# The experts' down product with the gated product as weights, on one Trainium2 core

## Chip, cores and metric

The kernel runs on one core of a Trainium2 chip. The metric is the device time of one execution in microseconds; lower is better. Names of engines: TensorE (PE in the rows; PEld is its weight load), VectorE (DVE), ScalarE (ACT), GpSimd (POOL), SyncE (SP, which starts transfers).

## What is computed

Four layers follow one another on x of 4 x 1024 tokens with 128 features. Each adds its result to x: banded attention, feed-forward, attention with a softmax over the heads, and the same feed-forward again. The change lies in the feed-forward, cut here to what matters:

```python
# x: 4096 tokens x 128, normalised; 32 experts with 64 inner features, 8 are chosen per token
g = einsum('th,eih->eti', x, expert_gate)
u = einsum('th,eih->eti', x, expert_up)
outs = einsum('eti,ehi->eth', silu(g) * u, expert_down)
final = sum over the 8 chosen experts of topk_w * outs
shared = (silu(x @ shared_gate.T) * (x @ shared_up.T)) @ shared_down.T
x = x + final + shared
```

## The kernel before

`feed_forward` runs twice, as ffn1 and ffn2, each time over 8 blocks of 512 tokens. All 32 experts are computed for all tokens, two at a time (a pair fills the 128 rows), with the share of experts that were not chosen set to zero. With the shared expert that makes 17 units in a block (`NU`), unit 0 of a block being the shared one, and 136 units in a stage. What follows calls the units of a block g = 0 to 16.

Float32 values are kept as two float16 parts, high and low, and each product is three matmuls: high by high, high by low, low by high. `product` (lines 112 to 116) does so with the expert's weights loaded into the array and 512 tokens streamed. For each unit:

- TensorE makes `gate` and `up` (three matmuls each, 128x512, features on the partitions).
- ScalarE makes `sg` = silu(gate) (L1443). GpSimd multiplies it by the tokens' shares of that expert into `sw` (L1332). VectorE multiplies `sw` by `up` into `hidden` (L1583, for the shared expert L1586).
- ScalarE copies `hidden` to its high part (L1448), VectorE subtracts to the low part (L1591), both into `h_parts`, which has three buffers.
- TensorE makes `down` from `h_parts` three units later (`LAG` = 3), and adds up all 17 units of a block in one PSUM bank, `down`.

After a block `down` holds the features on the partitions, and x has the tokens there. So ScalarE copies `down` to `dT` (`take_down`, L1453), TensorE turns it with four float32 transposes into a second bank, `back` (`turn_back`, L1389), and VectorE adds `back` to x (`add_back`, L1596).

The order is written out by hand, engine by engine, and engines wait for one another at counting semaphores. TensorE's loop does for each unit: gate, up, then down of the unit three before. So the last down of a block (g = 16) falls into g = 2 of the next block, behind up; after it stand the four transposes of the next block's shares (`turn_weights`, L1362). In g = 3 come gate, up and the first down of the new block, which in the kernel before waits for `dT_ready` (ScalarE has emptied the bank), and then `turn_back`. VectorE adds in its iteration g = 4. Its other work, the choice of experts for coming blocks (`route`), lies in g = 5 to 15, and in block 0 at double rate.

Of the kernel before, what the change touches and what calls it, by code (L numbers as in the profile page):

```python
# [16 lines left out]
ALU = mybir.AluOpType  # L17
ACT = mybir.ActivationFunctionType
AX = mybir.AxisListType

P = 128
B, S, E = 4, 1024, 128
# [5 lines left out]
BLK = 512  # L28
NBLK = T // BLK
TB = BLK // P  # L30
# [21 lines left out]
NPAIR = NEXP // 2  # L52
# [4 lines left out]
WSCALE = 16.0  # L57
ASCALE = 4.0
NU = NPAIR + 1
ONE = 1  # L60
# [51 lines left out]
def product(pe, out, w, i, hi, lo, start=True, stop=True):  # L112

    pe.matmul(out, w[:, i, 0, :], hi, start=start, stop=False)  # L114
    pe.matmul(out, w[:, i, 0, :], lo, start=False, stop=False)  # L115
    return pe.matmul(out, w[:, i, 1, :], hi, start=False, stop=stop)  # L116
# [1094 lines left out]
def feed_forward(nc, stage, c, x, mv, w_dram, stats_next, out=None):  # L1211
# [10 lines left out]
    LAG = 3  # L1222
    STATS = {NU - 1: range(2), 0: range(2, TB)}
    with Mem(nc, stage) as m:
# [10 lines left out]
        wide = m.sb("wide", [P, 2, NPAIR, BLK])  # L1235
        sg, sw = m.sb("sg", [P, 2, BLK]), m.sb("sw", [P, 2, BLK])
        h_parts = m.sb("h_parts", [P, LAG, 2, BLK], F16)
        dT = m.sb("dT", [P, BLK])
        stats = m.sb("stats", [P, TB, 6])
        gate, up, hidden = m.ps("gate", [P, 2, BLK]), m.ps("up", [P, 2, BLK]), m.ps("hidden", [P, 2, BLK])  # L1240
        down, back = m.ps("down", [P, BLK]), m.ps("back", [P, BLK])
# [6 lines left out]
        weights_ready, pt_ready, wT_ready = m.sem("weights_ready", "dve"), m.sem("pt_ready", "pe"), m.sem("wT_ready", "act")  # L1248
# [2 lines left out]
        gate_ready, up_ready, sg_ready = m.sem("gate_ready", "pe"), m.sem("up_ready", "pe"), m.sem("sg_ready", "act", 1)  # L1251
        sw_ready, h_ready = m.sem("sw_ready", "pool"), m.sem("h_ready", "dve", 1)
        high_ready, low_ready, down_done = m.sem("high_ready", "act"), m.sem("low_ready", "dve", 1), m.sem("down_done", "pe", LAG - 1)
        dT_ready, back_ready, added = m.sem("dT_ready", "act"), m.sem("back_ready", "pe"), m.sem("added", "dve")
        out_stored = m.sem("out_stored", "sp")
        block = m.ctx.enter_context(nc.Block())

# [8 lines left out]
        def part_of(unit):  # L1266

            return NPAIR if unit % NU == 0 else unit % NU - 1
# [65 lines left out]
        @block.tensor  # L1334
        def _(pe):
            m.start(pe, "pe")

            def turn(k):
                pe.wait_ge(xn_ready, ONE + k + 1)
                if k > 3:  # L1340
                    pe.wait_ge(xlow_ready, ONE + k - 3)
                    pe.wait_ge(xs_ready, ONE + k - 3)
                for j in range(TB):
                    last = pe.transpose(turned(k)[:, j * P:(j + 1) * P], xn[:, k % 2, j, :], c["ident"][:, :])  # L1344
                last.then_inc(turned_ready, 1)

            def logits_of(k):
                pe.wait_ge(xs_ready, ONE + k + 1)
                pe.wait_ge(logits_read, ONE + k)
                for j in range(TB):  # L1350
                    last = pe.matmul(logits[:, k % 2, j * NEXP:(j + 1) * NEXP], xs[:, k % 2, j * P:(j + 1) * P],  # L1351
                                     c["gate_w"][:, :], start=(j == 0), stop=True, skip_group_check=True)
                last.then_inc(logits_ready, 1)

            def turn_weights(k):
                pe.wait_ge(weights_ready, ONE + k + 1)
                if k > 0:
                    pe.wait_ge(wT_ready, ONE + k)
                if k > 2:
                    pe.wait_ge(added, ONE + k - 2)  # L1360
                for j in range(TB):
                    last = pe.transpose(back[0:NEXP, j * P:(j + 1) * P], weights[:, j, :], c["ident"][:, :])  # L1362
                last.then_inc(pt_ready, 1)

            def gate_of(unit):
                k, i = unit // NU, part_of(unit)
                xh, xl = xnT[:, 0, k * BLK:(k + 1) * BLK], xnT[:, 1, k * BLK:(k + 1) * BLK]
                pe.wait_ge(sg_ready, ONE + unit)
                product(pe, gate[:, unit % 2, :], c["gate_parts"], i, xh, xl).then_inc(gate_ready, 1)

            def up_of(unit):
                k, i = unit // NU, part_of(unit)
                xh, xl = xnT[:, 0, k * BLK:(k + 1) * BLK], xnT[:, 1, k * BLK:(k + 1) * BLK]
                pe.wait_ge(h_ready, ONE + unit)
                product(pe, up[:, unit % 2, :], c["up_parts"], i, xh, xl).then_inc(up_ready, 1)

            def down_of(unit):
                pe.wait_ge(low_ready, ONE + unit + 2)
                if unit % NU == 0:
                    pe.wait_ge(dT_ready, ONE + unit // NU)  # L1380
                product(pe, down[:, :], c["down_parts"], part_of(unit), h_parts[:, unit % LAG, 0, :], h_parts[:, unit % LAG, 1, :],
                        start=(unit % NU == 0), stop=(unit % NU == NPAIR)).then_inc(down_done, 1)

            def turn_back(k):
                pe.wait_ge(dT_ready, ONE + k + 1)
                pe.wait_ge(added, ONE + k)
                pe.wait_ge(wT_ready, ONE + min(k + 3, NBLK))
                for j in range(TB):
                    last = pe.transpose(back[:, j * P:(j + 1) * P], dT[:, j * P:(j + 1) * P], c["ident"][:, :])  # L1389
                last.then_inc(back_ready, 1)  # L1390

            for k in range(NBLK):
                turn(k)
                if k > 0:
                    logits_of(k - 1)
                if k == 3:
                    turn_weights(0)
            logits_of(NBLK - 1)
            pe.wait_ge(xlow_ready, ONE + NBLK)
            pe.wait_ge(xs_ready, ONE + NBLK)  # L1400
            for unit in range(UNITS + LAG):
                if unit < UNITS:
                    gate_of(unit)
                    if unit == 0:
                        pe.wait_ge(logits_read, ONE + NBLK + 1)
                    up_of(unit)
                if unit >= LAG:
                    down_of(unit - LAG)
                if turned_at(unit) is not None:
                    turn_weights(turned_at(unit))  # L1410
                if unit % NU == LAG and unit > NU:
                    turn_back(unit // NU - 1)
            turn_back(NBLK - 1)

        @block.scalar
        def _(act):
# [30 lines left out]
                act.wait_ge(down_done, ONE + unit)  # L1447
                act.activation(h_parts[:, unit % LAG, 0, :], hidden[:, unit % 2, :], ACT.Copy).then_inc(high_ready, 1)  # L1448

            def take_down(k):  # L1450
                act.wait_ge(down_done, ONE + (k + 1) * NU + LAG - 1)
                act.wait_ge(back_ready, ONE + k)
                act.activation(dT[:, :], down[:, :], ACT.Copy, scale=1 / WSCALE).then_inc(dT_ready, 1)  # L1453

            for k in range(NBLK):
                split_turned(k)
                if k > 0:
# [5 lines left out]
            for unit in range(UNITS):  # L1463
                gate_of(unit)
                if unit > 0:
                    high_part(unit - 1)
                if unit % NU == LAG - 1 and unit > NU:
                    take_down(unit // NU - 1)
                if turned_at(unit) is not None:
                    take_weights(turned_at(unit))  # L1470
            high_part(UNITS - 1)
            take_down(NBLK - 1)

        @block.vector
        def _(dve):
# [100 lines left out]
            def hidden_of(unit):  # L1576

                dve.wait_ge(up_ready, ONE + unit + 1)
                dve.wait_ge(low_ready, ONE + unit)
                h, upu = hidden[:, unit % 2, :], up[:, unit % 2, :]  # L1580
                if part_of(unit) < NPAIR:
                    dve.wait_ge(sw_ready, ONE + weighed_before(unit) + 1)
                    dve.tensor_tensor(h, sw[:, unit % 2, :], upu, ALU.mult).then_inc(h_ready, 1)  # L1583
                else:
                    dve.wait_ge(sg_ready, ONE + unit + 2)
                    dve.scalar_tensor_tensor(h, sg[:, unit % 2, :], 1 / WSCALE, upu, ALU.mult, ALU.mult).then_inc(h_ready, 1)  # L1586
# [4 lines left out]
                dve.tensor_tensor(h_parts[:, unit % LAG, 1, :], hidden[:, unit % 2, :], h_parts[:, unit % LAG, 0, :], ALU.subtract).then_inc(low_ready, 1)  # L1591

            def add_back(k):
                dve.wait_ge(back_ready, ONE + k + 1)
                xt = x[:, k * TB:(k + 1) * TB, :]
                dve.tensor_tensor(xt, xt, back[:, :].rearrange("p (t e) -> p t e", t=TB), ALU.add).then_inc(added, 1)  # L1596

            def stats_of(k, tiles):
                dve.wait_ge(added, ONE + k + 1)
# [22 lines left out]
            for unit in range(UNITS + 1):  # L1622
                if unit < UNITS:
                    hidden_of(unit)
                if unit > 0:
                    low_part(unit - 1)
                if unit % NU == LAG + 1 and unit > NU:
                    add_back(unit // NU - 1)
                k, pieces = pieces_at(unit)
                for piece in pieces:  # L1630
                    route(k, piece)
                if stats_next and unit > NU and unit % NU in STATS:
                    k = (unit + 1) // NU - 2
                    if k >= 0:
                        stats_of(k, STATS[unit % NU])
# [118 lines left out]
```

## Time and profile before

| | us |
|---|---|
| median of 3 runs (2033.71 to 2040.03) | 2039.27 |
| profiled execution, its time | 2041.47 |
| profiled execution, its span from first to last instruction | 2039.7 |
| TensorE busy | 1922.7 (94%) |
| VectorE busy | 1726.2 (85%) |
| GpSimd busy | 1512.7 (74%) |
| ScalarE busy | 1242.0 (61%) |

The two feed-forward stages lie at about 246 to 548 us and 1735 to 2040 us of the span. The mean granted clock of TensorE is 0.966 of full speed, and 1.00 inside the steady part of both. In the rows below a matmul's time runs from its start to its modelled end, so that the rows of a stream overlap; the pace is the distance between two starts.

### The profile page before, as it was taken

To read this page: it belongs to the slowest core of one execution; us is meant where nothing else is said; L and a number is where in the kernel's file an instruction comes from. 1 tells how busy PE (TensorE), PEld (TensorE's weight loads), DVE (VectorE), ACT (ScalarE), POOL (GpSimd) and SP (SyncE) were. 2 spreads that over 40 slices of the span, in tenths; PEclk is the share of its full clock that TensorE was granted. 3 is DMA by queue.
4 is the path that set the end of the run, shared out by engine and by line. 5 is a ranking of instruction groups with operands and counts; after the bars stand their busy time and mean duration, and the time that the engine had idled before them with its cause. 6 is when DMAs were issued, how large, how long until landed. Compare 5 with 4: busy or idle time off the path is not lost. (4 is left out here: it accounts for less than half of the span.)

```text
span 2039.7 us, 54384 instructions
## 1 busy us (share of the span) xinstructions
PE 1922.7 (94%) x21688; PEld 1277.0 (63%) x21688; DVE 1726.2 (85%) x2642; ACT 1242.0 (61%) x2225; POOL 1512.7 (74%) x1104
## 2 busy tenths in 40 slices
PE   5888799999889999999999999999999998899998
PEld 3566554444357777777777777777777776544443
DVE  6656688887689999999999999999999997788876
ACT  4446456666546666666666666666666665566665
POOL 5126035555359999999999999999999997256565
PEclk8989889999879999999999999999999999799999
DMA  7755167857120000000000000000000000578763
GB/s 194 205 126 128 31 125 132 157 126 134 68 79 13 14 9 18 9 14 14 13 15 9 17 10 14 13 11 16 6 10 6 9 6 2 87 157 152 131 130 60
DMA packets 119885, 125.83 MB, mean 62 GB/s; under 512 B 32208, under 2 KB 82272, under 8 KB 118896
## 3 DMA queue, kind: packets, MB, share of 16 engines
q1 hardware_dynamic: 114112, 117.65, 27.5%
q10 hardware_dynamic: 5520, 4.70, 0.8%
q8 instruction: 172, 2.82, 0.6%
q14 instruction: 81, 0.66, 0.1%
HBM read 101.71 MB, written 20.69 MB: 60 GB/s over the span
## 5 line engine op out<-in xcount | busy, mean ns | idle before, releaser
L1098 DVE TENSOR_REDUCE head_shift<-head_score 128x64 bf16<-128x1024 f32 x512 | 624.4, 1220 | 80.7 <-PE head_score L882 68.6
L1055 ACT ACTIVATE head_ex<-head_score 128x1024 f32<-128x1024 f32 x512 | 524.7, 1025 | 185.4 <-PE head_score L904 183.7
L839 POOL TENSOR_TENSOR head_half<-head_ex 128x1024 f32<-128x1024 f32 x256 | 604.1, 2360 | 40.7 <-ACT head_ex L1055 40.7
L1332 POOL TENSOR_TENSOR ffn_sw<-ffn_sg,ffn_wide 128x512 f32<-128x512 f32 x256 | 324.6, 1268 | 300.2 <-ACT ffn_sg L1443 283.0
L1105 DVE TENSOR_TENSOR head_ex<-head_ex,head_recp 128x1536 f32<-128x1536 f32 x256 | 446.7, 1745 | 4.2 <-ACT head_recp L1027 4.2
L914 PE MATMUL head_den<-head_half,c_ident 128*128 128x128 f32 x3072 | 385.4, 275 | 2.4 <-POOL head_half L840 2.4
L914 PEld LDWEIGHTS head_den<-head_half,c_ident 128*128 128x128 f32 x3072 | 363.4, 192 | 6.0 <-POOL head_half L840 2.6
L846 POOL TENSOR_TENSOR head_ex<-head_ex,head_recip 128x512 f32<-128x512 f32 x256 | 328.6, 1284 | 21.3 <-ACT head_recip L1029 12.9
L904 PE MATMUL head_score<-head_shift,c_identb 128*128 128x512 bf16 x1024 | 309.9, 384 | 17.9 <-DVE head_shift L1098 11.7
L882 PE MATMUL head_score<-att_b_HB,att_b_GR 96*128 96x256 f16 x2048 | 310.9, 274 | 1.1 <-issue 0.6
L897 PE MATMUL head_outp<-head_ex,att_b_vs 128*32 128x128 f32 x8192 | 276.5, 276 | 0.6 <-DVE head_ex L1105 0.6
L897 PEld LDWEIGHTS head_outp<-head_ex,att_b_vs 128*32 128x32 f32 x8192 | 208.1, 109 | 108.4 <-issue 107.4
L1583 DVE TENSOR_TENSOR ffn_hidden<-ffn_sw,ffn_up 128x512 f32<-128x512 f32 x256 | 178.1, 696 | 94.4 <-POOL ffn_sw L1332 85.5
L882 PEld LDWEIGHTS head_score<-att_b_HB,att_b_GR 96*128 96x128 f16 x2048 | 200.1, 98 | 81.5 <-ACT head_ex L1055 2.9
L1443 ACT ACTIVATE ffn_sg<-ffn_gate 128x512 f32<-128x512 f32 x272 | 162.1, 596 | 116.9 <-PE ffn_gate L116 115.7
L1448 ACT ACTIVATE ffn_h_parts<-ffn_hidden 128x512 f16<-128x512 f32 x272 | 162.2, 596 | 97.4 <-DVE ffn_hidden L1583 90.9
L840 POOL TENSOR_TENSOR head_half<-head_half 128x256 f32<-128x256 f32 x256 | 185.5, 725 | 20.1
L1024 ACT ACTIVATE head_lnd<-head_den 128x128 f32<-128x128 f32 x256 | 71.1, 278 | 206.8 <-PE head_den L914 206.8
L1591 DVE TENSOR_TENSOR ffn_h_parts<-ffn_hidden,ffn_h_parts 128x512 f16<-128x512 f32 x272 | 186.0, 684 | 0.1
L904 PEld LDWEIGHTS head_score<-head_shift,c_identb 128*128 128x128 bf16 x1024 | 72.2, 98 | 88.7 <-DVE head_shift L1098 79.6
L114 PE MATMUL ffn_down<-ffn_h_parts,c_down_parts 128*128 128x512 f16 x272 | 103.2, 379 | 3.3 <-DVE ffn_h_parts L1591 3.3
L114 PE MATMUL ffn_up<-ffn_xnT,c_up_parts 128*128 128x512 f16 x272 | 104.2, 383 | 0.4 <-DVE ffn_hidden L1583 0.2
(264 smaller groups left out, 2466.3 us busy)
## 6 DMA issues: line engine op xcount, KB each, us to landing
ffn_wide<-pair_weights SPq DMA_DIRECT2D x256, 256.0 KB, 9.7
band_v_windows<-a_values SPq DMA_DIRECT2D x24, 384.0 KB, 6.5
att_b_vs<-in_zero_f SPq DMA_DIRECT2D x2, 2176.0 KB, 9.0
a_values<-band_v_rows ACTq DMA_DIRECT2D x8, 512.0 KB, 5.7
a_keys<-band_parts_k SPq DMA_DIRECT2D x12, 295.5 KB, 2.8
att_a_HB<-a_keys SPq DMA_DIRECT2D x48, 73.9 KB
a_queries<-band_parts_q SPq DMA_DIRECT2D x12, 271.5 KB, 3.1
att_a_GR<-a_queries SPq DMA_DIRECT2D x12, 271.5 KB
```

Source lines behind the costliest of these rows:

```text
L114: pe.matmul(out, w[:, i, 0, :], hi, start=start, stop=False)
L839: ch.link(pool.tensor_tensor(hf, e[:, 0:8, :], e[:, 8:16, :], ALU.add))
L846: pool.tensor_tensor(e, e, recip[:, kt % 2, :][:, None, :].broadcast_to([P, NG, P]), ALU.mult).then_inc(rest_ready, 1)
L882: last = pe.matmul(score[:, h, g // 2, (g % 2) * GH * QS:(g % 2 + 1) * GH * QS].rearrange("p (a w) -> p a w", a=GH), GR[:, buf, g, kt * P: ...
L897: last = pe.matmul(outp[g * 32:(g + 1) * 32, 0:P], vs[:, buf * BT + kt, at:at + 32], ex[:, kt % RING, n, :], start=(kt == 0 and n4 == 0), ...
L904: last = pe.matmul(score[:, h, k, :].rearrange("p (a w) -> p a w", a=NH // 2), c["identb"][:, :], shift[:, h, :][:, None, :].broadcast_to( ...
L914: last = pe.matmul(den[:, 0:P], c["ident"][:, :], half[:, kt % 2, k, :], start=(i == 0), stop=(i == len(SLABS) - 1))
L1055: act.activation(ex[:, kt % RING, :, h * QS:(h + 1) * QS], score[:, h, :, :].rearrange("p k (a w) -> p (k a) w", a=NH // 2), ACT.Exp, scal ...
L1098: dve.tensor_reduce(shift[:, h, :], score[:, h, :, :].rearrange("p k (a w) -> p w k a", a=NH // 2), AX.XY, ALU.max, negate=True).then_inc( ...
L1105: dve.tensor_tensor(e, e, recp[:, 0:P][:, None, None, :].broadcast_to([P, NG, ON_DVE, P]), ALU.mult).then_inc(prob_ready, 1)
L1332: pool.tensor_tensor(sw[:, unit % 2, :], sg[:, unit % 2, :], wide[:, k % 2, i, :], ALU.mult).then_inc(sw_ready, 1)
L1591: dve.tensor_tensor(h_parts[:, unit % LAG, 1, :], hidden[:, unit % 2, :], h_parts[:, unit % LAG, 0, :], ALU.subtract).then_inc(low_ready, 1)
```

## The change

The down product changes its two operands. A piece of 128 tokens of `h_parts` is now loaded as weights, and the expert's down weights (128 columns) are streamed. The result has the tokens on the partitions and the features in the columns. A unit takes four pieces by three matmuls of 128 columns in place of three matmuls of 512. `take_down` and `turn_back` are gone, and with them `dT`, `dT_ready` and `back_ready`. VectorE adds `down` to x itself, with the scale in the same instruction. It does so in its iteration g = 2, between `hidden` of that unit and the low part of the unit before. The first down of a block waits for `added` instead of `dT_ready`.

```diff
             def down_of(unit):
+                w, i, parts = c["down_parts"], part_of(unit), h_parts[:, unit % LAG, :, :]
+                first, final = unit % NU == 0, unit % NU == NPAIR
                 pe.wait_ge(low_ready, ONE + unit + 2)
-                if unit % NU == 0:
-                    pe.wait_ge(dT_ready, ONE + unit // NU)
-                product(pe, down[:, :], c["down_parts"], part_of(unit), h_parts[:, unit % LAG, 0, :], h_parts[:, unit % LAG, 1, :],
-                        start=(unit % NU == 0), stop=(unit % NU == NPAIR)).then_inc(down_done, 1)
-
-            def turn_back(k):
-                pe.wait_ge(dT_ready, ONE + k + 1)
-                pe.wait_ge(added, ONE + k)
-                pe.wait_ge(wT_ready, ONE + min(k + 3, NBLK))
+                if first:
+                    pe.wait_ge(added, ONE + unit // NU)
                 for j in range(TB):
-                    last = pe.transpose(back[:, j * P:(j + 1) * P], dT[:, j * P:(j + 1) * P], c["ident"][:, :])
-                last.then_inc(back_ready, 1)
+                    high, low, out = parts[:, 0, j * P:(j + 1) * P], parts[:, 1, j * P:(j + 1) * P], down[:, j * E:(j + 1) * E]
+                    pe.matmul(out, high, w[:, i, 0, :], start=(first and j == 0), stop=False, skip_group_check=True)
+                    pe.matmul(out, high, w[:, i, 1, :], start=False, stop=False, skip_group_check=True)
+                    last = pe.matmul(out, low, w[:, i, 0, :], start=False, stop=final, skip_group_check=True)
+                last.then_inc(down_done, 1)
...
-                if unit % NU == LAG and unit > NU:
-                    turn_back(unit // NU - 1)
-            turn_back(NBLK - 1)
...
-            def take_down(k):
-                act.wait_ge(down_done, ONE + (k + 1) * NU + LAG - 1)
-                act.wait_ge(back_ready, ONE + k)
-                act.activation(dT[:, :], down[:, :], ACT.Copy, scale=1 / WSCALE).then_inc(dT_ready, 1)
...
             def add_back(k):
-                dve.wait_ge(back_ready, ONE + k + 1)
+                dve.wait_ge(down_done, ONE + (k + 1) * NU + LAG - 1)
                 xt = x[:, k * TB:(k + 1) * TB, :]
-                dve.tensor_tensor(xt, xt, back[:, :].rearrange("p (t e) -> p t e", t=TB), ALU.add).then_inc(added, 1)
+                dve.scalar_tensor_tensor(xt, down[:, :].rearrange("p (t e) -> p t e", t=TB), 1 / WSCALE, xt, ALU.mult, ALU.add).then_inc(added, 1)
...
                     hidden_of(unit)
+                if unit % NU == LAG - 1 and unit > NU:
+                    add_back(unit // NU - 1)
                 if unit > 0:
                     low_part(unit - 1)
-                if unit % NU == LAG + 1 and unit > NU:
-                    add_back(unit // NU - 1)
```

What stands on VectorE around the border of two blocks, from `hidden` of g = 1 on (`ffn_sw` by `ffn_up` is `hidden`, `ffn_h_parts` the low part, `x_tokens` is x). Before:

```order
L1583 TENSOR_TENSOR ffn_hidden<-ffn_sw,ffn_up 128x512
L1591 TENSOR_TENSOR ffn_h_parts<-ffn_hidden,ffn_h_parts 128x512
L1583 TENSOR_TENSOR ffn_hidden<-ffn_sw,ffn_up 128x512
L1591 TENSOR_TENSOR ffn_h_parts<-ffn_hidden,ffn_h_parts 128x512
L1583 TENSOR_TENSOR ffn_hidden<-ffn_sw,ffn_up 128x512
L1591 TENSOR_TENSOR ffn_h_parts<-ffn_hidden,ffn_h_parts 128x512
L1583 TENSOR_TENSOR ffn_hidden<-ffn_sw,ffn_up 128x512
L1591 TENSOR_TENSOR ffn_h_parts<-ffn_hidden,ffn_h_parts 128x512
L1596 TENSOR_TENSOR x_tokens<-x_tokens,ffn_back 128x512
```

And in the change (L1569 is `hidden`, L1577 the low part, L1582 the addition):

```order
L1569 TENSOR_TENSOR ffn_hidden<-ffn_sw,ffn_up 128x512
L1577 TENSOR_TENSOR ffn_h_parts<-ffn_hidden,ffn_h_parts 128x512
L1569 TENSOR_TENSOR ffn_hidden<-ffn_sw,ffn_up 128x512
L1582 SCALAR_TENSOR_TENSOR x_tokens<-ffn_down,x_tokens 128x512
L1577 TENSOR_TENSOR ffn_h_parts<-ffn_hidden,ffn_h_parts 128x512
```

The addition has moved up by two iterations and stands directly behind `hidden` of g = 2.

TensorE at the same border, from the last matmul of up in g = 3 to the gate of g = 4. Before:

```order
L116 MATMUL ffn_up<-ffn_xnT,c_up_parts 128x512
L114 MATMUL ffn_down<-ffn_h_parts,c_down_parts 128x512
L115 MATMUL ffn_down<-ffn_h_parts,c_down_parts 128x512
L116 MATMUL ffn_down<-ffn_h_parts,c_down_parts 128x512
L1389 MATMUL ffn_back<-c_ident,ffn_dT 128x128 x4
L114 MATMUL ffn_gate<-ffn_xnT,c_gate_parts 128x512
```

In the change:

```order
L116 MATMUL ffn_up<-ffn_xnT,c_up_parts 128x512
L1384 MATMUL ffn_down<-c_down_parts,ffn_h_parts 128x128
L1385 MATMUL ffn_down<-c_down_parts,ffn_h_parts 128x128
L1386 MATMUL ffn_down<-c_down_parts,ffn_h_parts 128x128
```

These three stand four times, twelve matmuls in a unit, and behind them comes the gate of g = 4 at once: the four transposes of L1389 are gone.

## Rows read from the trace of the kernel before

**Rows 1.** The page's first line: the span.

```profile
span 2039.7 us, 54384 instructions
```

**Rows 2.** Busy time by stretch: PE, PEld, DVE, ACT, POOL, clock, DMA share, GB/s.

```profile
1850.00:1950.00 100.00, 100.00 (x477) 46.70 (x475) 82.44 (x204) 61.53 (x107) 59.82 (x48) 1.00 0.78 141
```

**Rows 3.** Timeline of PE from block 3's first down: start, duration, instruction.

```profile
378.81 0.38 PE L114 MATMUL ffn_down<-ffn_h_parts,c_down_parts 128*128 128x512 f16 x1
...
379.45 0.60 PE L1389 MATMUL ffn_back<-c_ident,ffn_dT 128*128 128x128 f32 x4
379.89 0.38 PE L114 MATMUL ffn_gate<-ffn_xnT,c_gate_parts 128*128 128x512 f16 x1
...
383.77 0.38 PE L114 MATMUL ffn_gate<-ffn_xnT,c_gate_parts 128*128 128x512 f16 x1
```

**Rows 4.** Timeline of PE, first and last of 24 matmuls in the attention's start.

```profile
20.55 0.22 PE L361 MATMUL band_score<-c_a_parts,att_a_xnT 128*128 128x128 f16 x1
...
21.83 0.22 PE L363 MATMUL band_score<-c_a_parts,att_a_xnT 128*128 128x128 f16 x1
```

**Rows 5.** Instructions on the bank `down`: count, ns min/median/max, first and last start.

```profile
L114 PEld LDWEIGHTS ffn_down<-ffn_h_parts,c_down_parts x272: 95/98/98, 275.8 to 2034.1; 128*128 128x128 f16 x136
```

**Rows 6.** The same columns, for two lines of VectorE.

```profile
L1586 DVE SCALAR_TENSOR_TENSOR ffn_hidden<-ffn_sg,ffn_up x16: 685/695/697, 271.1 to 1999.9; 128x512 f32<-128x512 f32 x16
L1596 DVE TENSOR_TENSOR x_tokens<-x_tokens,ffn_back x16: 676/679/689, 316.2 to 2036.3; 128x512 f32<-128x512 f32 x16
```

**Rows 7.** Timeline of DVE at the start of block 3.

```profile
378.06 0.70 DVE L1583 TENSOR_TENSOR ffn_hidden<-ffn_sw,ffn_up 128x512 f32<-128x512 f32 x1 [0.55 <-POOL ffn_sw L1332]
378.66 0.68 DVE L1591 TENSOR_TENSOR ffn_h_parts<-ffn_hidden,ffn_h_parts 128x512 f16<-128x512 f32 x1
...
384.02 0.68 DVE L1596 TENSOR_TENSOR x_tokens<-x_tokens,ffn_back 128x512 f32<-128x512 f32 x1
```

**Rows 8.** Timelines of ACT and POOL at the start of block 3.

```profile
375.98 0.60 ACT L1443 ACTIVATE ffn_sg<-ffn_gate 128x512 f32<-128x512 f32 x1 [0.43 <-PE ffn_gate L116]
...
377.44 0.59 ACT L1453 ACTIVATE ffn_dT<-ffn_down 128x512 f32<-128x512 f32 x1
...
376.65 1.27 POOL L1332 TENSOR_TENSOR ffn_sw<-ffn_sg,ffn_wide 128x512 f32<-128x512 f32 x1 [0.62 <-ACT ffn_sg L1443]
```

**Rows 9.** Timelines of PE and DVE at the starts of blocks 1 and 7.

```profile
311.01 0.38 PE L114 MATMUL ffn_down<-ffn_h_parts,c_down_parts 128*128 128x512 f16 x1
...
311.12 0.68 DVE L1591 TENSOR_TENSOR ffn_h_parts<-ffn_hidden,ffn_h_parts 128x512 f16<-128x512 f32 x1
...
513.95 0.38 PE L114 MATMUL ffn_down<-ffn_h_parts,c_down_parts 128*128 128x512 f16 x1
...
514.25 0.68 DVE L1591 TENSOR_TENSOR ffn_h_parts<-ffn_hidden,ffn_h_parts 128x512 f16<-128x512 f32 x1
```

**Rows 10.** Timelines at the ends of ffn1 and ffn2.

```profile
544.45 0.38 PE L116 MATMUL ffn_down<-ffn_h_parts,c_down_parts 128*128 128x512 f16 x1
...
546.28 0.69 DVE L1596 TENSOR_TENSOR x_tokens<-x_tokens,ffn_back 128x512 f32<-128x512 f32 x1 [1.65 <-PE ffn_back L1389]
...
2034.51 0.38 PE L116 MATMUL ffn_down<-ffn_h_parts,c_down_parts 128*128 128x512 f16 x1
2034.93 0.60 ACT L1453 ACTIVATE ffn_dT<-ffn_down 128x512 f32<-128x512 f32 x1 [1.64 <-PE ffn_down L116]
...
2036.27 0.69 DVE L1596 TENSOR_TENSOR x_tokens<-x_tokens,ffn_back 128x512 f32<-128x512 f32 x1 [2.26 <-PE ffn_back L1389]
```

**Rows 11.** Timelines of PE and DVE in and just behind block 0 of ffn1.

```profile
289.11 0.61 PE L1362 MATMUL ffn_back<-c_ident,ffn_weights 128*32 128x128 f32 x4 [0.40 <-DVE ffn_weights L1564]
...
307.24 0.69 DVE L1586 SCALAR_TENSOR_TENSOR ffn_hidden<-ffn_sg,ffn_up 128x512 f32<-128x512 f32 x1
...
307.48 0.38 PE L116 MATMUL ffn_gate<-ffn_xnT,c_gate_parts 128*128 128x512 f16 x1
307.98 0.39 PE L114 MATMUL ffn_up<-ffn_xnT,c_up_parts 128*128 128x512 f16 x1
```

More of the change, by code:

```diff
@@ L1237, in feed_forward @@
         h_parts = m.sb("h_parts", [P, LAG, 2, BLK], F16)
-        dT = m.sb("dT", [P, BLK])
         stats = m.sb("stats", [P, TB, 6])
@@ L1253, in feed_forward @@
         high_ready, low_ready, down_done = m.sem("high_ready", "act"), m.sem("low_ready", "dve", 1), m.sem("down_done", "pe", LAG - 1)
-        dT_ready, back_ready, added = m.sem("dT_ready", "act"), m.sem("back_ready", "pe"), m.sem("added", "dve")
+        added = m.sem("added", "dve")
         out_stored = m.sem("out_stored", "sp")
@@ L1466, in _ @@
                     high_part(unit - 1)
-                if unit % NU == LAG - 1 and unit > NU:
-                    take_down(unit // NU - 1)
                 if turned_at(unit) is not None:
@@ L1471, in _ @@
             high_part(UNITS - 1)
-            take_down(NBLK - 1)
         @block.vector
```

## The prediction

> **What bounds the kernel now.** I read the page first, then the busy time by stretch, then the timelines of the four engines around one border between blocks. The span is 2039.7 us [rows 1]. In the middle of ffn2 TensorE is busy for all of a 100 us stretch, at a granted clock of 1.00, its full level of 2.4 GHz, while VectorE has 82 us of work and GpSimd 60 [rows 2]. So in both feed-forward stages TensorE's own stream is the bound, and every us of work or waiting that is put into that stream counts in full. The pace of the stream: from the gate at 379.89 to the gate at 383.77 lie 18 matmuls of 512 columns, 3.88 us or 0.2156 us each [rows 3]. A unit of nine is 1.94 us. Outside these stages nothing changes.
>
> **The down product.** Three matmuls of 512 columns take 3 x 0.2156 = 0.647 us. The new form, twelve matmuls of 128 columns with twelve weight loads, stands in the trace already: the values of the first attention are made with the same three-matmul pattern, and 24 of them start from 20.55 to 21.83, 1.28 us over 23 distances or 0.0557 us each [rows 4]. Twelve take 0.668 us. The columns are the same in number (1536), and each instruction adds a little over 2 ns, nine more of them per unit: +0.021 us. The weight load's own duration of 98 ns [rows 5] does not show in that pace. This counts in 232 of the 272 units. In block 0 of each stage VectorE sets the pace at several places: TensorE waits there for the shares at 289.11 (0.40 us idle) and for `hidden` before the up at 307.98, half a us behind the gate at 307.48 where 0.216 would do [rows 11]. A slower down uses up these waits, so I leave its 17 units out, and the last three of a stage, which wait for VectorE anyway. 232 x 0.021 = +4.9 us. Bounds: 0.019 per unit if the pace is 0.0555, which gives +4.3, and all of block 0 counted too, +5.6.
>
> **The transposes.** `turn_back` goes from TensorE's stream. It starts at 379.45 and the next gate at 379.89 [rows 3]: 0.44 us, seven times in each stage, 14 x 0.44 = -6.2 us. Its wait for `dT` cost nothing there, since it starts 0.64 us behind the first down as three matmuls ask. ScalarE's copy (0.59 us, [rows 8]) had cover, and is worth nothing inside the stage.
>
> **The wait that takes their place.** Before, ScalarE emptied the bank at 377.44 to 378.03 [rows 8], and the first down of the new block at 378.81 found it free [rows 3]. Now it waits until VectorE has added, and VectorE stands in `hidden` of g = 2 first. That one comes late: it needs `sg` (375.98), then `sw` on GpSimd (376.65, 1.27 us), and starts at 378.06 [rows 7, 8]. These are one chain from the gate, which the change leaves as it is. The instruction behind it starts at 378.66 [rows 7]. In the change this is the addition. No row has it in its new form; the nearest ones are the same operation on 128x512 with one PSUM operand, 0.695 us, and the present addition, 0.679 [rows 6]. I take 0.69, and 0.05 to reach TensorE, which is what it took from the end of L1586 at 307.93 to the up at 307.98 [rows 11]. So the down can start at 378.66 + 0.74 = 379.40. TensorE gets there at 378.81 + 0.02 (a longer down before it) = 378.83, and stands 0.57 us. Nothing can overtake: gate of g = 4 is queued behind it. That is the price for blocks 2 to 6, which look alike in both stages: 10 x 0.57 = 5.7 us. At block 1 it is 311.12 + 0.74 - 311.03 = 0.83, at block 7, where no `turn_weights` gives time, 514.25 + 0.74 - 513.97 = 1.02 [rows 9]; both stages, 2 x (0.83 + 1.02) = 3.7. Together +9.4 us. Bounds: 9.0 with 0.02 less per wait, 10.8 if the first weight load behind each wait, no longer hidden, adds its 98 ns [rows 5].
>
> The low part of g = 1 slides back by 0.6 us, to end at about 379.95. Its down is due at 379.40 + 0.668 + 1.29 = 381.36, so it has 1.4 us of cover. The addition at 384.02 [rows 7] leaves VectorE's iteration g = 4, where it held up nobody.
>
> **The ends.** Behind the last down of a stage the chain was ScalarE, TensorE, VectorE: from 2034.93 to the addition at 2036.27, 1.34 us [rows 10]. In ffn1 the last down ends at 544.83, and a hand-over of 0.04 as in ffn2 puts the start at 544.87; the addition came at 546.28, so 1.41. The addition now starts at once. The last down is 0.02 longer, twice. -2.7 us, bounds -2.5 and -2.8.
>
> **The sum.** +4.9 - 6.2 + 9.4 - 2.7 = +5.4 us. The profiled execution took 2041.47, 2.2 above the median of the runs, and would come to 2046.9. Against the median of 2039.27 that is **2044.7 us**, or 0.26% more. With the bounds: 4.3 - 6.2 + 9.0 - 2.8 = +4.3 to 5.6 - 6.2 + 10.8 - 2.5 = +7.7, so 2043.5 to 2047.
>
> **A rule weighed.** The row gives 0.0557 us for a matmul of 128 columns with its weight load, in a run of 24, at clock 1.00 [rows 4]. The Trainium skill, TensorE: Matmul & The Clock Gate, section Back-to-back issue gap, says that a stream of weight load and matmul pairs holds about 81 ns at 128 columns, and 56 is only the isolated gap. By that figure 232 units would take 12 x 0.081 - 0.647 = 0.325 us more each, an estimate of +75 us. The trace does not agree with it where it has the same pattern.
>
> **The rivals.**
> - *The addition does not hold TensorE.* If VectorE reached it in time, only the other terms would be left: 4.9 - 6.2 - 2.7 = -4.0 us, 2035.3, or -0.2%. VectorE's slack in the stretch speaks for it (82 of 100 us, [rows 2]); the order on the engine, behind a `hidden` that waits for GpSimd, speaks against [rows 7]. It decides when `hidden` of g = 2 starts 0.57 us earlier. 0.14.
> - *The wait is followed by more waits (slower).* The place is VectorE behind the addition: if the low part of g = 1, or `hidden` of g = 3, which is pushed back as well, comes too late for TensorE, each border is paid about twice. The point is 1.4 us of delay, and I see 0.6. Another +9.4 gives +14.8, 2054. A supply of instructions to TensorE that falls behind, with twice as many in these stages, would look alike in time. 0.18.
> - *The weight loads do not hide (slower).* With `h_parts` as weights a matmul would then take the load's 98 ns [rows 5]: 12 x 0.098 - 0.647 = 0.53 us per unit, +123 us, 2162. [Rows 4] speak against it. The section named above is for it in part. 0.04.
> - *Forecast,* +4.3 to +7.7: 0.58. *Something else:* 0.06.
>
> **How the numbers follow.** About 0.3%, 6.1 us, is what a measurement of this kernel can tell from no change. The forecast's 2044.7 lies just inside; of its 0.58 I put 0.40 within and 0.18 beyond. The first rival's 0.14 splits into 0.08 within and 0.06 faster, since runs of one kernel differ by some us. The two slower rivals give 0.22, and the rest is 0.02 each way. Faster 0.08, same 0.50, slower 0.42. The range reaches from near the first rival to near the second, 2037 to 2052; beyond it lie the third rival, half of the second and about a third of the first.
>
> **What would show it.** Twelve starts of down 0.0556 us apart, the next gate 0.668 behind the first. The addition right behind `hidden` of g = 2, about 0.69 us long. TensorE idle 0.5 to 1.0 us before the first down of each block from 1 on, 14 times, released by the addition and by nothing else. A border to border distance of 33.90 + 17 x 0.021 - 0.44 + 0.57 = 34.4 us (33.90 is 17 x 1.94 with two sets of transposes at 0.44). No idle time before L1384 elsewhere. I am wrong if down starts lie further apart than 0.06, if the wait is missing, or if waits follow it in g = 4 to 6.

## The result and the profile after

| | kernel before | changed kernel |
|---|---|---|
| median of 6 runs each, us | 2036.91 (2033.71 to 2040.03) | 2044.78 (2042.91 to 2047.26) |
| profiled execution, us | 2041.47 | 2043.80 |
| its span, us | 2039.7 | 2042.0 |

The ratio is 1.0037, 95% interval 1.0024 to 1.0050: slower by 7.9 us, a little more than the 5.4 us of the sum. A repetition on another occasion gave 1.0032, 1.0020 to 1.0045, or 7.2 us.

The line of busy times from the page of the changed kernel. TensorE has 2,384 more matmuls than before (24,072 against 21,688) and no more busy time.

```profile
PE 1921.4 (94%) x24072; PEld 1372.5 (67%) x24072; DVE 1725.7 (85%) x2642; ACT 1236.8 (61%) x2209; POOL 1513.9 (74%) x1104
```

Busy time of the same stretch as in [rows 2], in the changed kernel (PE, PEld, DVE, ACT, POOL, clock, DMA share, GB/s). TensorE was busy for all 100 us and now stands idle for 1.5, at the same clock:

```profile
1850.00:1950.00 100.00, 98.51 (x905) 62.99 (x903) 80.88 (x200) 59.59 (x102) 58.81 (x47) 1.00 0.77 140
```

Where it stands is in the timeline of PE from one set of share transposes (L1361) to the next, at the start of block 2 of ffn1. It answers to [rows 3]:

```profile
338.48 0.60 PE L1361 MATMUL ffn_back<-c_ident,ffn_weights 128*32 128x128 f32 x4
338.92 0.38 PE L114 MATMUL ffn_gate<-ffn_xnT,c_gate_parts 128*128 128x512 f16 x1
...
340.00 0.38 PE L116 MATMUL ffn_up<-ffn_xnT,c_up_parts 128*128 128x512 f16 x1
340.88 0.22 PE L1384 MATMUL ffn_down<-c_down_parts,ffn_h_parts 128*128 128x128 f16 x1 [0.50 <-DVE x_tokens L1582]
340.93 0.22 PE L1385 MATMUL ffn_down<-c_down_parts,ffn_h_parts 128*128 128x128 f16 x1
...
372.98 0.60 PE L1361 MATMUL ffn_back<-c_ident,ffn_weights 128*32 128x128 f32 x4
```

The first down starts 0.88 us behind the last matmul of up, where 0.216 is the pace: a wait of 0.66 us, and its releaser is the addition. (The row says 0.50, since it counts from the modelled end at 340.38.) The distance between the two sets of transposes is 34.50 us; before it was 33.89, from these rows:

```profile
343.18 0.60 PE L1362 MATMUL ffn_back<-c_ident,ffn_weights 128*32 128x128 f32 x4
...
377.07 0.60 PE L1362 MATMUL ffn_back<-c_ident,ffn_weights 128*32 128x128 f32 x4
```

VectorE and the load behind the wait, same place; this answers to [rows 7]:

```profile
339.44 0.70 DVE L1569 TENSOR_TENSOR ffn_hidden<-ffn_sw,ffn_up 128x512 f32<-128x512 f32 x1 [0.61 <-POOL ffn_sw L1331]
340.05 0.68 DVE L1582 SCALAR_TENSOR_TENSOR x_tokens<-ffn_down,x_tokens 128x512 f32<-128x512 f32 x1
...
340.85 0.10 PEld L1384 LDWEIGHTS ffn_down<-c_down_parts,ffn_h_parts 128*128 128x128 f16 x1 [0.97 <-issue]
340.88 0.10 PEld L1385 LDWEIGHTS ffn_down<-c_down_parts,ffn_h_parts 128*128 128x128 f16 x1
```

The addition stands behind a `hidden` that itself waited 0.61 us for GpSimd, and takes 0.68 us. The load comes 0.12 us behind its end. (The trace puts that load's wait down to "issue"; the matmul's row and the times name the addition.)

All such waits of the changed kernel, from the chain of waits of PE (total us, times, longest):

```profile
PE ffn_down L1384 <- DVE x_tokens L1582: 8.3, 14, 0.9
```

And the end of ffn2, against [rows 10]. The chain over ScalarE and the transposes is gone:

```profile
2038.35 0.22 PE L1386 MATMUL ffn_down<-c_down_parts,ffn_h_parts 128*128 128x128 f16 x1
2038.60 0.69 DVE L1582 SCALAR_TENSOR_TENSOR x_tokens<-ffn_down,x_tokens 128x512 f32<-128x512 f32 x1 [0.94 <-PE ffn_down L1386]
2039.32 0.37 SPq L1297 DMA_DIRECT2D out_x<-x_tokens  x1
```

**Two stages and the rest.** Runs of this kernel differ by some us in parts that no edit touches: what a profiled execution's span holds outside the two stages was 1472.6 to 1482.8 us over all kernels here. So the table in the next section measures the stages inside each trace as well, from the first gate matmul to the end of the last addition. Before, they took 278.68 (268.29 to 546.97) and 278.24 (1758.72 to 2036.96), together 556.92; in the changed kernel 281.92 and 281.14, together 563.06. That is +6.1 us.

### The profile page after: what moved, and what is told of

Same layout as the page of the kernel before. It is cut to its first block and busy times, and to the rows that moved or that the text cites. A ratio compares the mean times of both kernels' runs of the same rounds, so it can differ in the third digit from the quotient of the medians.

```text
span 2042.0 us, 59100 instructions
## 1 busy us (share of the span) xinstructions
PE 1921.4 (94%) x24072; PEld 1372.5 (67%) x24072; DVE 1725.7 (85%) x2642; ACT 1236.8 (61%) x2209; POOL 1513.9 (74%) x1104
## 5 line engine op out<-in xcount | busy, mean ns | idle before, releaser
L1569 DVE TENSOR_TENSOR ffn_hidden<-ffn_sw,ffn_up 128x512 f32<-128x512 f32 x256 | 178.2, 696 | 103.2 <-POOL ffn_sw L1331 97.5
L1384 PE MATMUL ffn_down<-c_down_parts,ffn_h_parts 128*128 128x128 f16 x1088 | 196.2, 219 | 11.5 <-DVE x_tokens L1582 8.3
L1386 PE MATMUL ffn_down<-c_down_parts,ffn_h_parts 128*128 128x128 f16 x1088 | 196.2, 219 | 0.0
L1385 PE MATMUL ffn_down<-c_down_parts,ffn_h_parts 128*128 128x128 f16 x1088 | 196.2, 219 | 0.0
L1577 DVE TENSOR_TENSOR ffn_h_parts<-ffn_hidden,ffn_h_parts 128x512 f16<-128x512 f32 x272 | 185.8, 683 | 0.1
```

The costliest lines, as they stand in the source:

```text
L1384: pe.matmul(out, high, w[:, i, 0, :], start=(first and j == 0), stop=False, skip_group_check=True)
L1385: pe.matmul(out, high, w[:, i, 1, :], start=False, stop=False, skip_group_check=True)
```

## The experiments

"Border" is the distance between two sets of share transposes of ffn1 (blocks 2 and 3), "unit" the mean pace of ten units inside block 3, "stages" the sum of both stages. The last two columns give the median of the timed runs and the ratio to the kernel before. That kernel was timed again on each occasion: its median was 2036.9 beside the changed kernel, 2036.3 beside experiments 1 to 4 and 2037.4 beside the others.

| kernel | border | unit | stages | median | ratio, 95% interval |
|---|---|---|---|---|---|
| before | 33.89 | 1.9425 | 556.9 | 2036.3 to 2037.4 | |
| changed | 34.50 | 1.965 | 563.1 | 2044.8 | 1.0037, 1.0024 to 1.0050 |
| changed, again | 34.50 | 1.965 | 563.1 | 2044.5 | 1.0032, 1.0020 to 1.0045 |
| addition first | 33.85 | 1.965 | 552.9 | 2032.6 | 0.9982, 0.9970 to 0.9994 |
| addition late | 35.09 | 1.965 | 571.2 | 2053.5 | 1.0082, 1.0068 to 1.0096 |
| before, down in 128 columns | 34.29 | 1.965 | 562.1 | 2043.3 | 1.0037, 1.0023 to 1.0050 |
| before, no transposes | 33.46 | 1.9425 | 549.0 | 2029.9 | 0.9961, 0.9949 to 0.9974 |
| changed, one wait | 34.43 | 1.965 | 562.2 | 2042.7 (one run) | |
| before, down in 256 columns | 34.02 | 1.950 | 558.8 | 2042.8 (one run) | |
| addition first, one wait | 33.84 | 1.965 | 552.9 | 2032.7 | 0.9970, 0.9957 to 0.9982 |

**1. The addition ahead of `hidden`.** If the wait is due to the addition's place, another place removes it.

```diff
+                if unit % NU == LAG - 1 and unit > NU:
+                    add_back(unit // NU - 1)
                 if unit < UNITS:
                     hidden_of(unit)
-                if unit % NU == LAG - 1 and unit > NU:
-                    add_back(unit // NU - 1)
```

> The changed kernel, with the addition in g = 2 placed ahead of `hidden` instead of behind it. Theory (TensorE waits for an addition that stands behind a late `hidden`): the down of g = 16 ends at 338.64 and VectorE is free at 338.75, `hidden` of g = 2 starts only at 339.44, so the addition fits into idle time of VectorE; all 14 waits of TensorE before the first down go, 2 x (0.91 + 5 x 0.66 + 1.10) = -10.6 us against the changed kernel, about 2034, or 0.9987 of the kernel before. Rival (the wait is only moved: the addition delays `hidden` of g = 2, and TensorE waits for that instead, or the time of the change lies in the down matmuls): within 3 us of the changed kernel, 2042 to 2048, ratio to before above 1.002.

Measured 2032.6, ratio 0.9982, against 2034 and 0.9987 expected; the rival's bound was 1.002. The timeline of DVE at the same border:

```profile
334.38 0.68 DVE L1577 TENSOR_TENSOR ffn_h_parts<-ffn_hidden,ffn_h_parts 128x512 f16<-128x512 f32 x1
334.98 0.68 DVE L1582 SCALAR_TENSOR_TENSOR x_tokens<-ffn_down,x_tokens 128x512 f32<-128x512 f32 x1
335.68 0.69 DVE L1569 TENSOR_TENSOR ffn_hidden<-ffn_sw,ffn_up 128x512 f32<-128x512 f32 x1
```

And that of PE, to the next border:

```profile
334.71 0.60 PE L1361 MATMUL ffn_back<-c_ident,ffn_weights 128*32 128x128 f32 x4
...
336.23 0.38 PE L116 MATMUL ffn_up<-ffn_xnT,c_up_parts 128*128 128x512 f16 x1
336.44 0.22 PE L1384 MATMUL ffn_down<-c_down_parts,ffn_h_parts 128*128 128x128 f16 x1
336.50 0.22 PE L1385 MATMUL ffn_down<-c_down_parts,ffn_h_parts 128*128 128x128 f16 x1
...
368.56 0.60 PE L1361 MATMUL ffn_back<-c_ident,ffn_weights 128*32 128x128 f32 x4
```

The addition fills what was VectorE's idle time before `hidden`, and ends at 335.66, 0.78 us before the first down, which follows the last up at the plain pace. `hidden` comes 2.28 us behind its up's first matmul (335.68 against 333.40), just as before (378.06 against 375.78). No wait of TensorE for the addition is left in this trace. The stages are 10.1 us shorter than in the changed kernel where 10.6 was expected; the missing half us lies in the first units of ffn2, and is looked at further down.

**2. The addition behind the low part as well.** If TensorE's stream is the bound, a later addition must cost what it is late.

```diff
                     low_part(unit - 1)
+                if unit % NU == LAG - 1 and unit > NU:
+                    add_back(unit // NU - 1)
```

> The changed kernel, with the addition in g = 2 placed behind the low part as well. Theory: TensorE's wait before the first down grows by the 0.60 us that VectorE's low part takes, 14 times: +8.4 us against the changed kernel, about 2053, ratio to before about 1.008. Rival (the place of the addition is not on the path, since later work makes up for it): unchanged, 2043 to 2047.

Measured 2053.5, ratio 1.0082. The wait grew as asked. PE:

```profile
371.46 0.38 PE L116 MATMUL ffn_up<-ffn_xnT,c_up_parts 128*128 128x512 f16 x1
...
372.93 0.22 PE L1384 MATMUL ffn_down<-c_down_parts,ffn_h_parts 128*128 128x128 f16 x1 [1.09 <-DVE x_tokens L1582]
```

The first down is 1.47 us behind the last up, 0.59 more than the changed kernel's 0.88; the border grew by 0.59 too. Nothing made up for it later.

**3. Only the down product in pieces.** The kernel before, with its operands as they were and everything else untouched:

```diff
-                product(pe, down[:, :], c["down_parts"], part_of(unit), h_parts[:, unit % LAG, 0, :], h_parts[:, unit % LAG, 1, :],
-                        start=(unit % NU == 0), stop=(unit % NU == NPAIR)).then_inc(down_done, 1)
...
+                for j in range(TB):
+                    high, low, out = parts[:, 0, j * P:(j + 1) * P], parts[:, 1, j * P:(j + 1) * P], down[:, j * E:(j + 1) * E]
+                    pe.matmul(out, w[:, i, 0, :], high, start=(first and j == 0), stop=False, skip_group_check=True)
+                    pe.matmul(out, w[:, i, 1, :], high, start=False, stop=False, skip_group_check=True)
+                    last = pe.matmul(out, w[:, i, 0, :], low, start=False, stop=final, skip_group_check=True)
+                last.then_inc(down_done, 1)
```

> The kernel before with its down product alone cut into twelve matmuls of 128 columns per unit; the expert's weights stay the loaded operand, the transposes and the order stay. Theory (a matmul of 128 columns costs a quarter of one of 512 and a little over 2 ns more, wherever its weights come from): +0.021 us in some 232 to 260 units, +5 to +5.5 us, ratio 1.0025. Rival A (loads of weights do not hide behind 128 columns in this stage): 98 ns each, over +100 us. Rival B (the extra pace of the changed kernel comes from loading the freshly written parts as weights): no change against the kernel before.

Measured 2043.3, ratio 1.0037 with an interval that holds the 1.0025 expected; the stages, free of the rest, grew by 5.2 us. The unit pace is 1.965, as in the changed kernel. Two gates, two units apart, show it:

```profile
381.20 0.38 PE L114 MATMUL ffn_gate<-ffn_xnT,c_gate_parts 128*128 128x512 f16 x1
...
385.13 0.38 PE L114 MATMUL ffn_gate<-ffn_xnT,c_gate_parts 128*128 128x512 f16 x1
```

Both rivals fall: the loads hide, and it does not matter which operand is loaded.

**4. Only the transposes away.** VectorE adds `dT` as it lies; the turning of the sum is left out.

```diff
-                if unit % NU == LAG and unit > NU:
-                    turn_back(unit // NU - 1)
-            turn_back(NBLK - 1)
...
-                act.wait_ge(back_ready, ONE + k)
+                act.wait_ge(added, ONE + k)
...
-                dve.wait_ge(back_ready, ONE + k + 1)
+                dve.wait_ge(dT_ready, ONE + k + 1)
...
-                dve.tensor_tensor(xt, xt, back[:, :].rearrange("p (t e) -> p t e", t=TB), ALU.add).then_inc(added, 1)
+                dve.tensor_tensor(xt, xt, dT[:, :].rearrange("p (t e) -> p t e", t=TB), ALU.add).then_inc(added, 1)
```

> The kernel before without its transposes: VectorE adds ScalarE's copy of the sum as it lies, features on the partitions, at its old place in g = 4. It leaves out the turning of the sum, so the output is not the reference's. Theory (0.44 us of TensorE's stream per block border, and 0.7 at each stage's end): 14 x 0.445 + 2 x 0.7 = -7.6 us, ratio 0.9963. Rival (the transposes lie in slack that GpSimd's chain leaves on TensorE): less than 2 us gained.

Measured 2029.9, ratio 0.9961; the border fell by 0.43 us, the stages by 7.9:

```profile
373.39 0.60 PE L1362 MATMUL ffn_back<-c_ident,ffn_weights 128*32 128x128 f32 x4
...
406.85 0.60 PE L1362 MATMUL ffn_back<-c_ident,ffn_weights 128*32 128x128 f32 x4
```

The transposes were all on the path.

**5. One wait instead of two.** In the changed kernel `low_ready` and then `added` stand ahead of the first down. `added` alone is enough from block 1 on, since VectorE makes that low part earlier.

```diff
-                pe.wait_ge(low_ready, ONE + unit + 2)
-                if first:
-                    pe.wait_ge(added, ONE + unit // NU)
+                if first and unit:
+                    pe.wait_ge(added, ONE + unit // NU)
+                else:
+                    pe.wait_ge(low_ready, ONE + unit + 2)
```

> The changed kernel, with one semaphore wait instead of two ahead of the first down of a block: `added` alone, which includes the low part of that unit in VectorE's order. In the changed kernel's trace the load behind the wait starts 0.12 us after the addition's end (340.73 to 340.85), where 0.05 was taken. Theory (the second wait instruction costs the rest): the load starts 0.05 after the addition's end, the distance between borders falls from 34.50 to 34.43. Rival (0.12 is the price of this releaser and this load, whatever the number of waits): 34.50 stays.

The border is 34.43 (340.73 to 375.16). DVE and PEld at the wait:

```profile
342.30 0.68 DVE L1583 SCALAR_TENSOR_TENSOR x_tokens<-ffn_down,x_tokens 128x512 f32<-128x512 f32 x1
...
343.03 0.10 PEld L1385 LDWEIGHTS ffn_down<-c_down_parts,ffn_h_parts 128*128 128x128 f16 x1 [0.90 <-DVE x_tokens L1583]
```

The load now starts 0.05 us behind the addition's end, not 0.12. A single run can't tell this 1 us from noise; the trace can.

**6. Six matmuls of 256 columns.** As experiment 3, with two pieces instead of four.

```diff
-                for j in range(TB):
-                    high, low, out = parts[:, 0, j * P:(j + 1) * P], parts[:, 1, j * P:(j + 1) * P], down[:, j * E:(j + 1) * E]
+                for j in range(2):
+                    high, low, out = parts[:, 0, j * 256:(j + 1) * 256], parts[:, 1, j * 256:(j + 1) * 256], down[:, j * 256:(j + 1) * 256]
```

> The kernel before with its down product cut into six matmuls of 256 columns per unit. Theory (a fixed 2.5 ns for each matmul, however wide, so 9 more gave the unit 0.0228 us): 3 more give 0.0076, a unit pace of 1.950 us in the trace, between 1.942 and 1.965. Rival (128 columns are a limit of their own, at which the weight load starts to show): 1.942 to 1.944, as with 512.

The unit pace is 1.950: three more matmuls cost 0.0075 us (1.9425 to 1.950), nine more 0.0225 (1.9425 to 1.965). The 0.0228 that the expectation took for nine was a little high. The cost goes by the number of matmuls, 2.5 ns each, and not by a limit at 128 columns. PE, one down of this kernel:

```profile
330.99 0.27 PE L1385 MATMUL ffn_down<-ffn_h_parts,c_down_parts 128*128 128x256 f16 x1
...
331.54 0.27 PE L1387 MATMUL ffn_down<-ffn_h_parts,c_down_parts 128*128 128x256 f16 x1
331.65 0.38 PE L114 MATMUL ffn_gate<-ffn_xnT,c_gate_parts 128*128 128x512 f16 x1
```

**7. Both: the addition first, and one wait.** The edits of experiments 1 and 5 together.

> The changed kernel with the addition ahead of `hidden`, and with the single wait. Theory (no wait is left at the borders, so the number of wait instructions ahead of the first down no longer matters): the same as with the addition moved alone, ratio to before 0.9982, border to border 33.84. Rival (each wait instruction costs TensorE's stream time even when it is met): 33.80 or less.

Border 33.84 and stages 552.9, the same as with the addition alone; the median is the same too, 2032.7 against 2032.6 (the two ratios come from different pools of runs, and their intervals overlap). A second wait costs something only where TensorE stands at it.

**8. The changed kernel again.** No edit; it shows how far a repetition differs.

> The changed kernel once more, on the chip of the others. Theory: stages longer by 5.2 us together than before, plus what runs of one kernel differ by in the untouched parts; ratio 1.0030 to 1.0037. A ratio of 1.001 or less would speak against 14 waits of 0.66 to 1.10 us.

Ratio 1.0032, borders and stages as in the first trace. So the stages are 6.1 us longer than before, not the 5.2 of the expectation, which is what experiment 3 gave for the down product alone. This trace has one pause that the first one lacks: in the last unit of block 6 of ffn2, 0.24 us between the first two matmuls of the gate, with no releaser in the row and away from any border. The first units of its two stages are 0.22 us shorter together, which hides that in the sum.

## Why the prediction was right

The sum said +5.4 us; the runs gave +7.9 and +7.2, the stages of the trace +6.1. The median of 2044.78 stands beside the 2044.7 forecast, but that agreement owes something to chance: the median of before fell from 2039.27 to 2036.91 as more runs came in. Against that, the size of the change was underestimated by about 2 us: +7.9 is just above the upper bound of the sum (+7.7), though its interval of +4.9 to +10.2 reaches down to the +5.4. It also lies a little beyond the 0.3% within which the prediction counted a change as none, on the side that had been given the smaller chance (slower 0.42, same 0.50). Two of the recorded bounds don't follow from their own terms: 232 x 0.019 is +4.4, not +4.3, and 14 waits each 0.02 shorter make +9.1, not +9.0, so the lower bound should read +4.5.

Point by point, with what the traces measured:

| step | foretold | measured |
|---|---|---|
| down product, per unit | +0.021 | +0.0225 (experiments 3 and 6) |
| down product, 232 units | +4.9 | +5.2 |
| transposes, 14 borders | -6.2 | -6.1 (33.89 to 33.46 in experiment 4) |
| wait at blocks 2 to 6, each | 0.57 | 0.66 |
| wait at block 1; block 7 | 0.83; 1.02 | 0.91; 1.10 |
| all 14 waits | +9.4 | +10.6 |
| the two ends | -2.7 | -2.7 |
| sum | +5.4 | +7.0 |

- **What bounds the kernel.** Right, and shown from both sides: 0.59 us later at VectorE made a border 0.59 us longer (experiment 2), and what was taken from TensorE's stream came back in full (experiment 4). 0.44 us is what four transposes take of that stream, and the border shrank by 0.43.
- **The down product.** Right in kind, 7% too small per unit. I took 0.0557 from 23 distances, which rounds the last digit, and 0.2156 for the wide ones, and wrote their difference as 0.021; the fixed part of a matmul is 2.5 ns, and nine times that is 0.0225. The weight loads hide behind 128 columns over whole stages. The rule of the Trainium skill that was weighed (TensorE: Matmul & The Clock Gate, section Back-to-back issue gap), 81 ns in a stream of load and matmul pairs, is not what this trace shows; the 56 ns that the same page gives for the isolated gap is. Twelve matmuls of the changed kernel, each with its load, take 0.670 us from the first to the next gate, 55.8 ns each.
- **The wait.** Right in place, number and releaser: 14 waits, all for the addition, none behind them. Moving the addition ahead of `hidden` removed them and 10.1 us of the stages (563.1 to 552.9), and the ratio to the kernel before fell from 1.0037 to 0.9982, by 11 us. Each of the 14 was 0.08 to 0.09 us longer than foretold. Experiment 5 puts 0.07 of it on the second of the two wait instructions. The rest, 0.03, lies between the load and its matmul (340.85 to 340.88); I had it only in the upper bound, with 98 ns. The five other waits in front of L1384 (3.1 us in all) stand in the last three units of a stage, and the kernel before has the same five (3.3 us).
- **The ends.** From the gate of g = 6 of block 7 to the end of the last addition: 28.05 to 26.96 in ffn1 and 27.35 to 26.25 in ffn2, so -1.1 each, which is -1.35 and eleven longer downs (the last three of a stage wait for VectorE).
- **Block 0.** Left out of the sum, with reason: from the gate of g = 6 of block 0 to that of g = 3 of block 1 a stage is only 0.02 to 0.03 us longer, where fourteen longer downs would make 0.3, so the waits there do take them up. But the terms above make +7.0 and the stages show +6.1. The missing 0.9 us lies in the first six units of each stage, 0.30 us shorter in ffn1 (12.23 to 11.93) and 0.62 in ffn2 (12.49 to 11.87). TensorE enters them at the lower of its two clock levels, 1.2 GHz, and the granted clock goes from 0.50 to 1.00 some us behind the first gate. By the clock record of each trace that is, in ffn1, 4.25 us behind it in the kernel before and 3.25 in the changed one, and in ffn2 5.45 and 3.14. The kernel of experiment 4 does in that stretch exactly what the kernel before does; in ffn1 its clock rose at 3.16, and it took 11.87. Here is the same place, 2 to 4 us behind the first gate of ffn1, before and in experiment 4 (columns as in [rows 2]); TensorE is busy throughout in both, at a different clock:

```profile
270.29:272.29 2.00, 2.00 (x6) 0.76 (x5) 1.18 (x3) 0.41 (x1) 0.00 (x0) 0.50 1.01 183
267.84:269.84 2.00, 2.00 (x8) 0.81 (x7) 1.18 (x3) 0.71 (x2) 0.00 (x0) 0.71 1.02 167
```

And 2 to 4 us behind the first gate of ffn2, before and in the changed kernel:

```profile
1760.72:1762.72 2.00, 2.00 (x6) 0.76 (x5) 1.18 (x3) 0.41 (x1) 0.00 (x0) 0.50 0.98 141
1760.15:1762.15 2.00, 2.00 (x8) 0.83 (x7) 1.18 (x3) 0.72 (x2) 0.00 (x0) 0.72 1.03 168
```

Over the twenty stages of the ten traces (before, changed, and the eight experiments) the first six units take the longer the later the clock rises, to within 0.02 us: from 11.49 us (rise at 2.35) to 12.58 (rise at 5.62), level only between rises at 4.0 and 4.8. So the missing 0.9 us is a difference of the clock. What sets the moment of its rise stays open. In ffn1 it differs between kernels that are the same up to the first gate; in ffn2 it came early (2.35 to 3.14) in the four traces with the waits at the borders and late (4.99 to 5.62) in the six without, so the change may have a part in it that no run tells apart.

- **Rival one**, that the addition doesn't hold TensorE: false for the change as made. It is what experiment 1 builds: 0.9982 of the kernel before is -3.7 us, against -4.0 worked out.
- **Rival two**, further waits: none in the trace. A border is the sum of its terms: 33.89 + 17 x 0.0225 - 0.44 + 0.66 = 34.49, where 34.50 was measured and 34.4 foretold.
- **Rival three**, loads that don't hide: false, experiments 3 and 6.

The rest of +7.9 against +6.1 is within the interval of the ratio (+4.9 to +10.2 us).

The version with the addition first beats both kernels: 0.9982 (0.9970 to 0.9994) and, with one wait, 0.9970 (0.9957 to 0.9982) of the kernel before, and 4.0 us less in the stages. Of these, 3.6 are what the change is worth once its wait is gone: -6.1 for the transposes and -2.7 for the ends, against +5.2 for the smaller matmuls. The rest is the earlier rise of the clock in the first units.

## What to carry to other kernels

A copy that is removed from between two engines may have been what set a buffer free early: ask at which place in its own order the new reader stands, and what that place waits for, before counting the copy's time as won. Here the same addition one step earlier in VectorE's order, in time that was idle anyway, turned +6.1 us in the stages into -4.0. Splitting matmuls costs by their number, small but on the path of a TensorE-bound stage in full. And where runs differ by more than the effect, compare repeated distances inside the traces (34.50 against 33.89, eight times in the two stages) rather than two medians.

## What the runs showed of the hardware beyond that

- Here a second semaphore wait ahead of a TensorE instruction cost 0.07 us when TensorE stood at it (0.12 against 0.05 from the release to the load), and nothing measurable when both were met on arrival (border 33.85 and 33.84).
- Matmuls of 128, 256 and 512 columns, each with a weight load of 128x128, take a fixed 2.5 ns each beyond their columns (unit pace 1.965, 1.950 and 1.9425 with 18, 12 and 9 matmuls and the same columns), with the load of 98 ns hidden at all three sizes at full clock, whether the loaded operand is a constant or has just been written by ScalarE and VectorE.
